# Rows gathered once in sorted order, and the low halves of expert weights made by GpSimd, in a fused graph-attention and top-2 expert kernel

## The reference, cut to what matters

```python
# N = 6250 tokens, D = 256, 4 heads of 64, 8 experts, top 2
xt = (layernorm(x) @ weight).reshape(-1, 4, 64)
alpha = softmax(leaky_relu(einsum(xt[src], attn_l) + einsum(xt[dst], attn_r), 0.01))
x = x + broadcast(einsum('nh,nhd->nd', alpha[:n], xt[dst[:n]]))       # the same for all heads
t = layernorm(x)
probs = softmax(t @ router_w.T); rw, re = top_k(probs, 2); rw = rw / rw.sum()
out = t
for e in range(8):
    out = out + combine[:, e] * (gelu(t @ w1[e] + b1[e]) @ w2[e] + b2[e])
return x + out
```

## Time and profile before

| what | us |
| --- | --- |
| three runs | 495.93, 503.22, 503.90 |
| median | 503.22 |
| profiled execution, whole | 506.39 |
| its span, first to last instruction | 504.6 |
| busy in the span: PE | 382.1 (76%) |
| DVE | 342.0 (68%) |
| ACT | 276.1 (55%) |
| POOL | 244.4 (48%) |

### The profile page before, as it was taken

How to read it: one execution, slowest core, us unless ns; L and a number is a source line. 1 busy time by engine, 2 the same in 40 slices (tenths; PEclk the granted TensorE clock), 3 DMA queues, 4 the chain that set the end, 5 groups by cost and what they waited for, 6 DMA issues and landing times.

```text
span 504.6 us, 11001 instructions
## 1 busy us (share of the span) xinstructions
PE 382.1 (76%) x3546; PEld 334.2 (66%) x3546; DVE 342.0 (68%) x1160; ACT 276.1 (55%) x715; POOL 244.4 (48%) x241
## 2 busy tenths in 40 slices
PE   3597874898978782645883999798787787889991
PEld 2486764887868672534772988687576676769990
DVE  2549595597979888793662768576465655668871
ACT  3157542455454645752642577476564656569870
POOL 8468884475757510005465445545445354533332
PEclk9998987997979887756996899989999999999996
DMA  4263535374646443222233222212212122121110
GB/s 151 64 164 117 173 111 161 114 202 145 202 139 199 146 119 94 76 78 58 64 87 87 68 76 67 75 56 68 73 47 73 54 66 66 54 66 43 45 54 19
DMA packets 30085, 48.21 MB, mean 96 GB/s; under 512 B 5720, under 2 KB 22898, under 8 KB 30028
## 3 DMA queue, kind: packets, MB, share of 16 engines
q0 software_dynamic: 10896, 29.61, 20.0%
q1 hardware_dynamic: 18378, 17.32, 11.7%
q10 hardware_dynamic: 756, 0.58, 0.4%
HBM read 34.42 MB, written 13.07 MB: 94 GB/s over the span
## 4 chain that ended last, share of the span: by engine, by line
PE 38%; issue 14%; another core or an unknown queue 13%; ACT 13%; DVE 11%; POOL 5%; DMA 2%; DVEq 1%; ACTq 0%; POOLq 0%
PE bank L1490 9%; PE bank L1299 8%; PE bank L1512 7%; PE bank L1302 3%; POOL out_dram L560 3%; ACT h L732 3%; PE bank L1290 3%; PE bank L1323 2%; PE bank L1428 2%; DVE h_lo L1225 2%; PE bank L1505 2%; DVE acc L1243 1%; ACT acc L613 1%; ACT work L720 1%
## 5 line engine op out<-in xcount | busy, mean ns | idle before, releaser
L512 POOL DMA_INDIRECT acc<-in_x_dram,index x98 | 114.8, 1171 | 57.9 <-ACT work L603 30.9
L732 ACT ACTIVATE h<-bank,b_col 128x128 f32<-128x128 f32 x250 | 78.1, 365 | 85.2 <-PE bank L1490 58.1
L551 POOL DMA_INDIRECT work<-token_table,order x76 | 75.0, 987 | 98.0 <-DVE order L1175 52.5
L1490 PE MATMUL bank<-work,w_hi 128*128 128x128 f16 x1000 | 103.4, 223 | 20.1 <-issue 17.2
L1243 DVE SCALAR_TENSOR_TENSOR acc<-bank,work,acc 128x256 f32<-128x256 f32 (+1 forms) x125 | 60.4, 483 | 77.8 <-remote 41.8
L1490 PEld LDWEIGHTS bank<-work,w_hi 128*128 (+1 forms) x1000 | 83.5, 100 | 25.9 <-issue 20.0
L1490 PE MATMUL bank<-work,w_lo 128*128 128x128 f16 x500 | 93.8, 223 | 2.5 <-issue 2.5
L560 POOL DMA_INDIRECT out_dram<-acc,order x49 | 48.9, 998 | 95.2 <-DVE acc L1243 90.3
L1299 PE MATMUL bank<-w_ext,work 128*128 128x260 f32 x196 | 62.0, 445 | 14.7 <-ACT work L596 7.2
L1512 PE MATMUL bank<-w_hi,h_lo 128*128 (+1 forms) x250 | 69.0, 276 | 1.7 <-issue 1.7
L1512 PE MATMUL bank<-w_lo,h_hi 128*128 (+1 forms) x250 | 69.0, 276 | 0.9 <-issue 0.9
(11 more groups left out here) (210 smaller groups left out, 712.0 us busy)
## 6 DMA issues: line engine op xcount, KB each, us to landing
acc<-in_x_dram SPq DMA_DIRECT2D x42, 112.0 KB
work<-in_L_ffn_w_dram SPq DMA_DIRECT2D x16, 256.0 KB
token_table<-row_out SPq DMA_DIRECT2D x28, 133.0 KB
token_table<-row_out SPq DMA_DIRECT2D x3, 931.0 KB
acc<-in_x_dram,index POOLq DMA_INDIRECT x98
work<-token_table,order POOLq DMA_INDIRECT x76
acc<-in_x_dram SPq DMA_DIRECT2D x1, 784.0 KB
out_dram<-acc,order POOLq DMA_INDIRECT x49
```

The lines of the kernel that those rows point to most:

```text
L512: nc.gpsimd.indirect_dma_start(out=xds[:, t % RING, n, :], out_offset=None, in_=x, in_offset=bass.IndirectOffsetOnAxis(ap=index[:, n, t:t ...
L551: nc.gpsimd.indirect_dma_start(out=rows[:, k % ROWS_RING, :], out_offset=None, in_=table, in_offset=bass.IndirectOffsetOnAxis(ap=order[:, ...
L732: last = nc.scalar.activation(h32[:, i % RINGS, f * P:(f + 1) * P], bank[i % RINGS][:, f * P:(f + 1) * P], ACT.Gelu, bias=bias_of(f), scal ...
L1490: last = nc.tensor.matmul(bank[i % RINGS][:, f * P:(f + 1) * P], first_weights(i, lo, c, f), x2T[:, r, half, c * P:(c + 1) * P], start=(m ...
```

## The change

1. **Rows are gathered once.** `rows` now holds all 49 tiles (and a dummy tile), and is also the sum: `accumulate` adds into its first 256 columns. `gather_rows` runs 49 times, not 76, and gather k waits only for gather k - 16. In GpSimd's queue all gathers stand before the first scatter. The two additions of a tile become one (`add_normal`), `acc` and its clearing go.
2. **Extras by a register.** The turned rows of all tiles are kept (`x2T`), and an extra reads its tile's by a number in a register (`sorted_columns`). It no longer has a gather, a normalisation, a transpose or a split. `ITEMS` is now 24 tiles (48 items), the 27 extras, 25 tiles (50 items). Item i prepares tile i + 2 while there are tiles left. A scatter of the first 24 tiles waits for the last extra (`done`). ScalarE normalises three tiles of four and VectorE the fourth. The experts' numbers are loaded to registers in two parts, and the extras' tiles after the order is out.
3. **Low halves on GpSimd.** For 14 of the 16 pieces ScalarE first scales the piece in place, then writes the high half, and GpSimd subtracts (`piece_lo`). VectorE keeps the two head pieces. The load of a later piece waits for GpSimd's count.

The core of the diff:

```diff
-ITEMS = [(k, None) for k in range(EXTRAS)] + [(EXTRAS + q, n) for q in range(TILES) for n in range(2)]
+AHEAD = 24
+ITEMS = ([(q, n) for q in range(AHEAD) for n in range(2)] + [(k, None) for k in range(EXTRAS)]
+         + [(q, n) for q in range(AHEAD, TILES) for n in range(2)])
...
+            def piece_lo(n):
+                which, e = piece(n)
+                pool.wait_ge(s_piece_hi, n + 1)
+                nc.gpsimd.tensor_tensor(w_lo[which][:, e, :, :].rearrange("p k n -> p (k n)"), stage[:, n % STAGE, :],
+                                        w_hi[which][:, e, :, :].rearrange("p k n -> p (k n)"), ALU.subtract).then_inc(s_piece_lo, 1)
+
             for g in range(GROUPS):
                 for t in range((g + 1) * GT + EARLY, min((g + 2) * GT + EARLY, TILES)):
                     gather(t)
+                if g > 0:
+                    for n in pieces_of(g - 1):
+                        piece_lo(n)
...
             def gather_rows(k):
-                column = TILES + k if k < EXTRAS else k - EXTRAS
-                if k >= ROWS_RING:
-                    pool.wait_ge(s_acc, SUMS[last_item(k - ROWS_RING)])
-                elif k >= FIRST_ROWS:
-                    pool.wait_ge(s_acc, SUMS[last_item(k - FIRST_ROWS)])
+                at_least(pool, s_rows[k % ROWS_RING], 16 * (k // ROWS_RING))
                 nc.gpsimd.indirect_dma_start(
-                    out=rows[:, k % ROWS_RING, :], out_offset=None, in_=table,
+                    out=rows[:, k, :], out_offset=None, in_=table,
...
             def scatter(q):
-                pool.wait_ge(s_acc, SUMS[last_item(EXTRAS + q)])
+                pool.wait_ge(s_acc, done(q))
...
-            for k in range(PREPS):
+            for k in range(TILES):
                 gather_rows(k)
-                if k - SCATTER_LAG >= EXTRAS:
-                    scatter(k - SCATTER_LAG - EXTRAS)
-            for q in range(TILES - SCATTER_LAG, TILES):
+            for q in range(TILES):
                 scatter(q)
...
             def piece_hi(n):
...
+                if n >= HEAD_PIECES:
+
+                    nc.scalar.activation(stage[:, n % STAGE, :], stage[:, n % STAGE, :], ACT.Copy, scale=SPLIT).then_inc(s_scaled_piece, 1)
+                    act.wait_ge(s_scaled_piece, n - HEAD_PIECES + 1)
...
-            def add_rows(k):
-                q = k - EXTRAS
-                at_least(dve, s_acc, min(sums.n, SUMS[EXTRAS - 1]))
-                sums(nc.vector.tensor_tensor(acc[:, q, :], acc[:, q, :], rows[:, k % ROWS_RING, 0:D], ALU.add))
-
             def add_normal(k):
-                q = k - EXTRAS
-                sums.ready()
-                sums(nc.vector.tensor_tensor(acc[:, q, :], acc[:, q, :], x2[:, k % X2_RING, :], ALU.add))
-                last_sum[q] = sums.n
+
+                dve.wait_ge(s_x2_turn if by_vector(k) else s_x2, normalised(k, by_vector(k)))
+                sums(nc.vector.tensor_tensor(rows[:, k, 0:D], rows[:, k, 0:D], x2[:, k % X2_RING, :], ALU.add))
...
+            def sorted_columns(i, half, c):
+
+                k, n = ITEMS[i]
+                if n is None:
+                    return x2T[:, bass.ds(tiles[k], 1), half, c * P:(c + 1) * P].rearrange("p t d -> p (t d)")
+                return x2T[:, k, half, c * P:(c + 1) * P]
```

More of the change, by code:

```diff
@@ L342, in build @@
         s_extra = sem("extra_tiles_in_sbuf")
-        s_zero = sem("accumulators_zeroed")
         v_o = sem("vector_order_chain")
@@ L403, in load_edges, with prep_of @@
             eng.dma_start(index[:, n, :], edge[0:P * TILES].rearrange("(p t) -> p t", t=TILES)).then_inc(s_index, 16)
[L405 to L412, removed]
+        def prep_of(i):
+            return i + READY if i + READY < TILES else None
+        SUMS, ADDED = {}, {k: k + 1 for k in range(READY)}
+        count = READY
+        for i in range(len(ITEMS)):
             if i >= LAG:
@@ L415, in build @@
                 SUMS[i - LAG] = count
-            if n in (None, 0) and EXTRAS <= k + 2 < PREPS:
-                count += 2
+            if prep_of(i) is not None:
+                count += 1
+                ADDED[prep_of(i)] = count
         for i in range(len(ITEMS) - LAG, len(ITEMS)):
@@ L420, in build, with by_vector, normalised, done @@
             SUMS[i] = count
+        def by_vector(k):
+            return k % TURN == TURN - 1
+        def normalised(k, vector):
+            return sum(by_vector(j) == vector for j in range(k + 1))
+        def done(q):
+            return SUMS[LAST_EXTRA if q < AHEAD else EXTRAS + 2 * q + 1]
         block = ctx.enter_context(nc.Block())
@@ L958, in step @@
                     edge_stats(nxt + 1)
-                if not more and now:
-                    for n in pieces_of(g):
-                        piece_lo(n)
                 if past:
@@ L1463, in first_addresses @@
                         address(first_weights(i, lo, c, f), True)
+                if extra(i) and f == 0:
+                    for half in range(2):
+                        address(sorted_columns(i, half, c), False)
             def second_addresses(i):
@@ L1524, in load_experts, with load_tiles @@
                     experts[q] = [(word, at), (word, at + 3)]
+            def load_tiles():
+                pe.wait_ge(s_extra, 1)
+                _, words = nc.values_load_multi_w_load_instructions(
+                    extra_tile[0:1, :], engines=[ENG.PE], min_val=0, max_val=64 ** PACK - 1,
+                    skip_runtime_bounds_check_because="tiles' numbers, or the dummy's, as the cuts give them")
+                for k in range(EXTRAS):
+                    tiles[k] = words[k // PACK], 6 * (k % PACK)
@@ new lines, in _ @@
+            load_experts(0, FIRST_WORDS)
+            for step in range(2):
+                unpack(0, step)
+            for f in range(KT):
+                for c in range(KT):
+                    first_addresses(0, f, c)
+            for k in range(READY):
+                sorted_transpose(k)
+            for i in range(len(ITEMS)):
+                if i == FIRST_EXTRA - 2:
+                    load_tiles()
+                if i == LAST_EXTRA - 1:
+                    load_experts(FIRST_WORDS, WORDS)
+                first_item(i)
+                if prep_of(i) is not None:
+                    sorted_transpose(i + READY)
```

306 lines of the change are left out of this document (155 added, 151 removed).

## The result

The changed kernel took **542.01 us** (median of 4 runs, 539.72 to 544.06) against 501.55 us for the kernel before (4 runs, 495.93 to 503.9): ratio **1.085**, 95% interval 1.073 to 1.096. The forecast was 490 us, in a range of 462 to 525. It missed in sign and in range. The profiled execution took 544.06 us, against 506.39 before.

What follows compares the result with a forecast made beforehand. It took late TensorE signals during GpSimd's back-to-back DMAs as the bound: 506.4 - 57.4 - 6.2 - 1.2 - 2 + 31 + 19.5 + 3 = 493.1, forecast as 490 us because the profiled execution is 3.2 above the median; range 462 to 525.

Steps and rivals of the forecast that it cites:

- The bound: Experts' stage: TensorE's signals arrive late while GpSimd issues DMAs back to back, 57.4 us lost.
- The gathers' row: Experts' stage: 49 gathers back to back for 61 us, at 0.63 us lost each, cost 31 us.
- dear run: Rival, experts' stage: long DMA runs hold TensorE all the time, 1.2 us a DMA, 528 us; chance 0.22.
- The scatters' row: After the last extra: 31 scatters back to back, at 0.63 us lost each, cost 19.5 us.
- TensorE stays the bound at 1.66: First 47 items, each with a preparation: 1.66 us an item on TensorE, VectorE near, nothing added.
- the fourth rival: Preparations at every item make VectorE the bound, 1.8 us an item, 7 us over 47; no chance given.
- Register loads: Loads of the experts' numbers, two in the stage: 1.5 us each, +3, between 0 and 6.
- Transposes: Extras without preparation: 27 pairs of transposes go from TensorE's path, -6.2 us.
- Edge stage and order: Low halves: -1.2 us in the last step, -2 over five groups; order priced at nothing.
- the rival of the held edge stage: GpSimd's subtractions make each edge-stage group 3 us longer, +15, 507 us; chance 0.14.

Runs made afterwards that it cites:

- e10: Kernel before, with a GpSimd clear of 512 elements after each of its 76 gathers and 49 scatters: 453.34 us, ratio 0.901.
- e12: Changed kernel with 512-element clears after each gather and scatter, VectorE normalising every second tile instead of every fourth: 464.03 us, ratio 0.923.
- e15: Changed kernel with 512-element clears after each gather and scatter, ScalarE normalising four items ahead instead of three: 460.79 us, ratio 0.922.
- e2: Changed kernel, the scatter of tile q also waiting for the q-th sum after the last extra item: 518.08 us, ratio 1.050.
- e1: Changed kernel, each gather from the ninth on waiting for the sum of the item eight before: 486.75 us, ratio 0.982.
- e7: Changed kernel, gathers spaced by waits for sums, and a GpSimd clear of 512 elements after each scatter: 460.27 us.

## Why the prediction was wrong, point by point

**The bound.** Right that GpSimd's DMAs back to back, and no engine's work, cost the kernel before 57 us; e10 got 48 of its 501 back with clears alone. But "what TensorE signals arrives late" is only how it begins: in the earlier trace rows a sum starts 3.4 us after its matmul. A few us into a run TensorE itself slows to an instruction each 0.70 us, and that costs far more than a late signal. The trace of before shows these steps in the run of the earlier trace rows; I read DVE and ACT there, and not TensorE:

```profile
264.06 0.28 PE L1512 MATMUL bank<-w_lo,h_hi 128*128 128x256 f16 x1 [0.37 <-issue]
...
264.77 0.27 PE L1512 MATMUL bank<-w_lo,h_hi 128*128 128x256 f16 x1 [0.22 <-issue]
...
265.49 0.28 PE L1512 MATMUL bank<-w_hi,h_lo 128*128 128x256 f16 x1 [0.45 <-issue]
```

**The gathers' row: 31 us forecast, 58.5 measured.** This is the step that failed. I took 0.63 us a DMA, "from 48 DMAs, the row with most of them", but those 48 stand 104.6 / 48 = 2.18 us apart on average, in fours with rests between. A price for a spaced DMA was put on a DMA in a row. The unbroken run of twelve was the only row of the same kind, and its 1.2 gives 59. The "dear run" rival had the mechanism, the place and the size; I gave it 0.22, because it rested on one run of DMAs. Its border was also wrong: at 0.75 us a DMA the two rows cost 36.8 + 22.0 = 58.8 us, which gives 498 and not 503; 503 needs 0.82. The number of DMAs behind a price counts for less than whether they stand as the changed ones will.

**The scatters' row: 19.5 forecast, 31.4 measured,** 25 in a row: again the dear rival's figures (25 scatters, 30 us), by the same mistake.

**"TensorE stays the bound at 1.66".** 1.84 instead, +7.7 us: the size of the fourth rival, not its engine. I had compared VectorE's busy time, and not looked at when ScalarE's normalisation comes in relation to the transposes (e12, e15).

**Register loads,** 3 forecast, 1.2 measured. **Transposes** as forecast: items without a preparation take 1.43.

**Edge stage and order,** -3.2 forecast, -2.6 measured in the profiled pair, a hit that proves little: the same edge code brought the first gather between 218.6 and 230.2 us in different runs (e2, e1). A subtraction took 1.16 us, in a pair of 2.27, where I took 1.3. The Trainium skill (GPSIMD Engine Reference, section 3.1, Elementwise) led to an estimate of 1.1 us plus dispatch; the trace agrees. The groups stayed near 24 us, so the rival of the held edge stage did not come.

**The drain,** +5.1, forecast nowhere.

From 493.1: + 27.5 + 11.9 + 7.7 - 1.8 + 5.1 + 0.6 = 544.1, the profiled 544.06. Of 51 us, 39 are one misjudged price. With 1.2 a DMA the sum would have been 528, outside my range, which cut off half of that rival.

## What to carry to other kernels

Count GpSimd's indirect DMAs beside TensorE's work by rate, not by number: on this kernel one in 1.7 us is free, one in 1.55 costs, one in 1.25 to 1.44 stops TensorE almost entirely, and the least change that restores it is a wait for progress or a useless instruction between them. A change that batches such DMAs, or removes the waits that spread them, needs that check first; a clear of 512 elements after each is the cheap test of whether a kernel suffers. And when a price comes from the trace, take it from rows that stand as the new ones will, even if there is only one.

## What the runs showed of the hardware

- While indirect DMAs of GpSimd stand 1.25 us apart, TensorE's signals come late first (3.4 us in the earlier trace rows), and after some 6 us of DMAs (scatters from 424.35, the first idle "issue" at 430.1) it starts only one instruction each 0.70 us; the other engines' own work keeps its durations (Gelu pairs 0.62, sums 0.48 us).
- By estimate an indirect DMA takes 1.39 to 1.40 us of whatever is shared, and an item 0.33 (68.7 us for 49, 34.8 for 25, 5.17 for three of each); e7 and e10 show these prices to be up to 5% too high. The loss is the same for 64 or 128 rows and for 256 or 1024 bytes a row, and plain DMAs of GpSimd do not cause it at 0.56 us each, in rows of up to ten. The Trainium skill (SBUF — State Buffer, section SBUF: two separate sides) says that DMAs and compute operations cannot slow each other at SBUF's ports. These runs do not contradict that, since bytes made no difference, but the slowing itself is there, so it must lie elsewhere. It also outlasts the transfers: TensorE was slow for 6 us after the last gathered data (291.7 to 297.7). Where it lies, the runs do not tell: the trace has no record of what TensorE waits for. That stays open.
- A VectorE instruction with two operands in SBUF waits while GpSimd subtracts operands from there: 2.60 us for 0.20. One with a single operand does not (0.42 as ever).
- GpSimd's closing drain differs by 5.1 us between two programs with the same last DMAs (3.8 and 8.9).
